# First pooling of a graph U-Net: turning the adjacency in 2-byte pairs of destinations, and picking the byte with two products per block

## The reference, cut to what matters

```python
def gcn_conv(x, W, b, src, dst, mask, n):
    h = x @ W
    ew = mask.astype(h.dtype)
    deg = 1.0 + jax.ops.segment_sum(ew, dst, num_segments=n)
    dinv = jax.lax.rsqrt(deg)
    norm = dinv[src] * dinv[dst] * ew
    agg = jax.ops.segment_sum(h[src] * norm[:, None], dst, num_segments=n)
    return agg + h * (1.0 / deg)[:, None] + b

def topk_pool(x, w, src, dst, mask, k):
    score = jnp.tanh((x * w).sum(-1) / jnp.sqrt((w * w).sum()))
    _, idx = jax.lax.top_k(score, k)
    n = x.shape[0]
    new_id = jnp.zeros((n,), jnp.int32).at[idx].set(jnp.arange(k, dtype=jnp.int32))
    kept = jnp.zeros((n,), bool).at[idx].set(True)
    mask2 = mask & kept[src] & kept[dst]
    return (x[idx], new_id[src], new_id[dst], mask2, idx)

# in the U-Net, i = 0, 1, 2:
    x = gcn_conv(x, dn_W[i], dn_b[i], src, dst, mask, n)
    x = jax.nn.relu(bn_train(x, dn_g[i], dn_beta[i]))
    k = int(RATIO * n)            # 3125 -> 1562 -> 781 -> 390
    x2, src2, dst2, mask2, idx = topk_pool(x, pool_w[i], src, dst, mask, k)
```

## Time and profile before

| | |
|---|---|
| median of 3 runs | 1019.72 us (1019.04 to 1021.31) |
| the profiled execution | 1018.97 us |
| its span, first to last instruction | 1017.0 us |
| granted TensorE clock, mean over the span | 0.978 |
| half turn, first product to last copy | 657.08 to 682.24 us |
| full turn, first product to last degree sum | 692.11 to 710.90 us |

### The profile page before, as it was taken

The page is one execution under the profiler, slowest core; times in us unless marked ns, Lnnn a source line. Parts: engine busy times, 40 slices in busy tenths (PEclk is TensorE's granted clock), DMA queues, the critical chain, the costliest instruction groups (busy, mean ns, idle before and its releaser), DMA issues.

```text
span 1017.0 us, 17626 instructions
## 1 busy us (share of the span) xinstructions
PE 907.3 (89%) x7247; PEld 601.0 (59%) x7247; DVE 590.3 (58%) x1557; ACT 401.2 (39%) x895; POOL 62.9 (6%) x84
## 2 busy tenths in 40 slices
PE   2347999999999999999999999998989687899997
PEld 1345666776765556775575576566545444456555
DVE  4789999995965972465212128384453464516311
ACT  0788999993554010165102013275214402122100
POOL 4000000000000000000000000404002200120000
PEclk9979999999899999999999999999999699999999
DMA  5010000003960002003000000784214300151002
GB/s 157 17 29 1 3 1 1 2 2 155 398 256 1 1 1 65 1 1 129 1 1 1 1 1 19 241 265 120 102 36 128 89 1 2 47 212 69 1 1 66
DMA packets 39505, 66.66 MB, mean 66 GB/s; under 512 B 3525, under 2 KB 27310, under 8 KB 38902
## 3 DMA queue, kind: packets, MB, share of 16 engines
q1 hardware_dynamic: 34464, 45.94, 13.1%
q0 software_dynamic: 4064, 17.86, 5.4%
q10 hardware_dynamic: 886, 1.61, 0.5%
HBM read 29.09 MB, written 36.32 MB: 64 GB/s over the span
## 4 chain that ended last, share of the span: by engine, by line
PE 61%; DVE 27%; ACT 4%; DMA 3%; issue 2%; POOL 1%; ACTq 0%; DVEq 0%; SPq 0%; POOLq 0%
PE psum L3121 26%; DVE region L1083 7%; PE psum L2616 7%; DVE region L1076 7%; PE psum L2504 7%; PE psum L2845 4%; DVE region L1681 2%; PE psum L2581 2%; PE psum L2409 2%; PE psum L2434 2%; PE psum L3069 1%; PE psum L2967 1%; DMA nodebuf<-in_x 1%; POOL region L839 1%; ACT nodebuf L2014 1%
## 5 line engine op out<-in xcount | busy, mean ns | idle before, releaser
L3121 PE MATMUL psum<-adj,region 128*128 128x448 fp8e4 (+1 forms) x1200 | 202.6, 329 | 1.1 <-DVE region L1920 1.0
L3121 PEld LDWEIGHTS psum<-adj,region 128*128 128x128 f16 x1200 | 116.5, 98 | 81.0 <-DVE region L1920 1.7
L2434 PE MATMUL psum<-region 128*128 128x200 bf16 (+2 forms) x1176 | 111.2, 229 | 27.3 <-DVE region L1083 19.0
L2434 PEld LDWEIGHTS psum<-region 128*128 128x128 bf16 x1176 | 93.4, 99 | 61.7 <-DVE region L1083 33.4
L1083 DVE TENSOR_TENSOR region<-iota_key,region 128x1200 bf16<-128x1200 bf16 x147 | 92.6, 702 | 0.0
L2071 ACT ACTIVATE adj<-psum 128x400 fp8e4<-128x400 f32 x196 | 86.5, 520 | 14.8 <-PE psum L2438 14.2
L2409 PE MATMUL psum<-adj,region 128*128 128x448 fp8e4 x350 | 92.1, 356 | 0.0
L1076 DVE TENSOR_TENSOR region<-iota_lo,region 128x3072 bf16<-128x3072 bf16 x49 | 86.9, 1774 | 5.2 <-PE psum L2438 5.0
L1948 DVE SCALAR_TENSOR_TENSOR region<-psum,unfit,region 128x448 f32<-128x448 f32 (+3 forms) x34 | 20.1, 622 | 107.7 <-PE psum L3121 98.4
L1681 DVE CAST region<-psum 128x512 fp8e4<-128x512 f32 (+2 forms) x87 | 46.6, 598 | 57.3 <-PE psum L2947 27.6
L3121 PE MATMUL psum<-region 128*128 128x448 fp8e4 (+3 forms) x452 | 76.8, 329 | 3.4 <-DVE region L1920 3.4
(11 more groups left out here) (376 smaller groups left out, 1268.6 us busy)
## 6 DMA issues: line engine op xcount, KB each, us to landing
both_table<-adj SPq DMA_DIRECT2D x1, 10000.0 KB, 28.7
adj_table<-adj SPq DMA_DIRECT2D x1, 10000.0 KB, 54.8
region<-dk_dram SPq DMA_DIRECT2D x2, 1568.0 KB, 7.3
both_table<-region SPq DMA_DIRECT2D x1, 2704.0 KB, 9.6
half_table<-region SPq DMA_DIRECT2D x2, 832.0 KB, 5.3
xs_dram<-nodebuf SPq DMA_DIRECT2D x1, 1600.0 KB, 5.2
nodebuf<-xs_dram SPq DMA_DIRECT2D x1, 1600.0 KB, 6.2
half_table<-region SPq DMA_DIRECT2D x2, 768.0 KB, 6.0
```

Source lines behind the costliest of these rows:

```text
L2434: pe.matmul(psum[:, q % BUILD_BANKS, i * KEYS + k0:i * KEYS + k1], hot_lo[:, r, c, j, :, i], hot_key[:, r, c, j, k0:k1, i], start=(n == 0) ...
L3121: last = pe.matmul(psum[:, b if b < BLOCKS else LAST_BANK, 0:width], here[:, t, k, :], rows, start=(t == 0 and k == 0), stop=(t == n_src - ...
```

## The change

- `adj` rows are read as 2-byte elements: destinations 2j and 2j+1 travel together. A row of 3200 bytes is 1600 elements, 12 tiles of 128 and one of 64 (`PAIR_TILES` 13, `PAIR_TAIL` 64).
- Half turn: 169 PE transposes of 2-byte elements (BF16 view, `ident16`) instead of 325 products. ACT and DVE copy them as 16-bit integers; a unit is 5 blocks (group 0) or 8 blocks (groups 1 and 2) of 128 elements; 27 units instead of 82. `half_table[0]` has 1664 lines of 3328 bytes, one for both destinations of a pair. It is still stored in six DMAs, now of 6 and 7 tiles.
- POOL gathers lines `node >> 1` (`node_of[:, 2]`), 3328 bytes each instead of 1664, 13 times 128 of them as before. They lie in other places of SBUF (`dst_block`).
- Full turn: of a gathered pair one byte is wanted. DVE makes two masks from the identity, `only_odd` (identity times the node's lowest bit) and `only_even` (the rest). For each block PE makes two products, the even bytes with one and the odd bytes with the other, in one PSUM sum: 338 products instead of 169.
- Both turns of this level use two banks per engine (3 and 4 for ACT, 5 and 7 for DVE), four in all.
- The skip sums move. Pass 0 (64 were left ahead of the half turn) goes 50 ahead of group 0 and 14 ahead of group 1; pass 1, now in bank 6, goes 14 ahead of group 2 and 36 between the turns. ACT's `take_skip(0)` moves behind the half turn, and the first degree sum waits for `take_skip(1)`, since it writes bank 6 too.

The second pooling keeps its form.

```diff
-TURN_BANKS = 3
+TURN_BANKS = (((3, 4), (5, 7)), ((0, 1, 2), (3, 4, 5)))
+PAIR_TILES = 13
+PAIR_TAIL = PAD // 2 - (PAIR_TILES - 1) * P
+def pair_ones():
+    return [(d, 1) for d in range(PAIR_TILES)]
+def pair_twos():
+    return [(d, min(2, PAIR_TILES - 1 - d)) for d in range(0, PAIR_TILES - 1, 2)] + [(PAIR_TILES - 1, 1)]
 def half_units(level):
+    if level == 0:
+        return [(g, d, count, 0, n) for g, (m0, n) in enumerate(store_groups(0)) for d, count in (pair_twos() if n <= 4 else pair_ones())]
...
 def half_parts(level):
+    if level == 0:
+        return ((0, 6), (6, PAIR_TILES))
...
+        half_table = [dram("half_table0", (PAIR_TILES * P, ROW[1] // 2), I32), dram("half_table1", (LEVEL_TILES[1] * P, ROW[2] // 4), I32)]
...
-        SKIP_PASSES = ((0, 0, 3, 0), (0, 3, 4, 7), (0, 4, BLOCKS, 0), (1, 0, 3, 0), (1, 3, 4, 3))
+        SKIP_PASSES = ((0, 0, 3, 0), (0, 3, 4, 6), (0, 4, BLOCKS, 0), (1, 0, 3, 0), (1, 3, 4, 3))
...
+                    if lv == 0:
+                        pool.wait_ge(pairs_known, 1)
                     for n in range(tiles_up):
-                        gather(dst_block(lv, n).bitcast(I32), half_table[lv], node_of[:, lv, n:n + 1], rows_gathered[n // 2])
+                        gather(dst_block(lv, n).bitcast(I32), half_table[lv], node_of[:, 2 - lv, n:n + 1], rows_gathered[n // 2])
...
+                    if level == 0:
+                        dve.wait_ge(nodes_known, 1)
+                        v.tensor_scalar(node_of[:, 2, :].bitcast(I32), node_of[:, 0, :].bitcast(I32), 1, None, ALU.arith_shift_right).then_inc(pairs_known, 1)
...
+                        dve.wait_ge(nodes_stored, DMA * len(NODE_STORES[0]))
...
+                        step(v.tensor_tensor(only_odd, every, odd.rearrange("p (t o) -> p t o", o=1).broadcast_to((P, packed_tiles, P)), ALU.mult))
+                        v.tensor_tensor(only_even, every, only_odd, ALU.subtract).then_inc(pairs_known, 1)
...
-                        take_skip((0, 2, 3)[below])
+                        if below > 0:
+                            take_skip((0, 2, 3)[below])
...
                                 if below == 0:
+                                    take_skip(0)
                                     take_skip(1)
...
+            SKIP_TURN, SKIP_LAST = ((86, 136), (136, 150)), 14
...
-                skip_sums(skips, SKIP_PICK[below][3], skip_sizes(skips))
+                if below > 0:
+                    skip_sums(skips, SKIP_PICK[below][3], skip_sizes(skips))
...
                 for u in range(turns(below)):
                     e, k, bank, _, _ = turn_unit(below, u)
+                    if below == 0 and (u == 0 or u < len(halves) and halves[u][0] != halves[u - 1][0]):
+                        pe.wait_ge(nodes_known, level)
+                        g = halves[u][0]
+                        if g < len(SKIP_TURN):
+                            skip_sums(0, *SKIP_TURN[g])
+                        if g == 2:
+                            skip_sums(1, 0, SKIP_LAST)
                     if u == len(halves):
                         pe.wait_ge(nodes_known, level)
                         if below == 0:
-                            skip_sums(1, 0, skip_sizes(1))
+                            skip_sums(1, SKIP_LAST, skip_sizes(1))
+                            pe.wait_ge(pairs_known, 2)
...
+                                if below == 0:
+                                    lanes = P if d < PAIR_TILES - 1 else PAIR_TAIL
+                                    at = ((d - d0) * n + m - m0) * P // 2
+                                    last = pe.transpose(psum[0:lanes, bank, at:at + P // 2].bitcast(BF16),
+                                                        src_block(0, m).bitcast(BF16)[:, d * P:d * P + lanes], ident16[:])
+                                    continue
...
+                            if below == 0:
+                                pairs = dst_block(0, n).bitcast(FP8).rearrange("p (s i) -> p s i", i=2)[:, m * P:(m + 1) * P, :]
+                                to = psum[:, bank, (m - m0) * P:(m - m0 + 1) * P]
+                                pe.matmul(to, pairs[:, :, 0], only_even[:, n, :], start=True, stop=False)
+                                last = pe.matmul(to, pairs[:, :, 1], only_odd[:, n, :], start=False, stop=True)
+                                continue
```

More of the change, by code:

```diff
@@ L30 @@
 U32 = mybir.dt.uint32
+U16 = mybir.dt.uint16
 P = 128
@@ L217, in gnn_kernel @@
         adj_table = dram("adj_table", (LEVEL_TILES[0] * P, ROW[0] // 4), I32)
-        half_table = [dram(f"half_table{lv}", (LEVEL_TILES[lv] * P, ROW[lv + 1] // 4), I32) for lv in range(PACKINGS)]
+        half_table = [dram("half_table0", (PAIR_TILES * P, ROW[1] // 2), I32), dram("half_table1", (LEVEL_TILES[1] * P, ROW[2] // 4), I32)]
         both_table = [dram(f"both_table{lv}", (LEVEL_TILES[lv] * P, BOTH_ROW[lv]), F32) for lv in range(PACKINGS)]
@@ L365, in gnn_kernel @@
         packed_adj.append(packed_adj[2])
-        half_at = ((3808, 7808), (6618, 8282), (6618, 7514))
+        half_at = ((3380, 7540), (6618, 8282), (6618, 7514))
+        only_even, only_odd = (r34(832 * k, 832).bitcast(F16).rearrange("p (t n) -> p t n", n=P) for k in range(2))
         node_rows = [r34(0, LEVEL_TILES[lv] * NODE_ROW[lv]).rearrange("p (t f) -> p t f", f=NODE_ROW[lv]) for lv in range(3)]
@@ L492, in gnn_kernel @@
         nodes_known = sem("nodes_known")
+        pairs_known = sem("pairs_known")
         rows_moved = relu_done = sem("rows_moved_or_relu_done")
@@ L609, in dst_block @@
         def dst_block(level, n):
-            at, words = gathered_dst[level]
-            return region12[:, at + n * words:at + (n + 1) * words]
+            if level == 1:
+                return region12[:, 3850 + n * 224:3850 + (n + 1) * 224]
+            return r34(3380 + 832 * n, 832) if n < 9 else region12[:, 832 * (n - 9):832 * (n - 8)]
         def up_block(level, t):
@@ L632, in turn_unit @@
             k = (before(ACT_TURNS, level) if e == 0 else before(DVE_TURNS, level)) + u // 2
-            bank = TURN_BANKS * e + k % TURN_BANKS
+            banks = TURN_BANKS[level][e]
+            bank = banks[u // 2 % len(banks)]
+            if level == 0 and u < len(halves):
+                g, d0, count, at, n = halves[u]
+                lanes = P if d0 + count < PAIR_TILES else PAIR_TAIL
+                to = half_rows(0, g).bitcast(U16)[0:lanes, d0:d0 + count, :]
+                return e, k, bank, to, psum[0:lanes, bank, 0:count * n * P // 2].bitcast(U16).rearrange("p (d n) -> p d n", d=count)
             if u < len(halves):
@@ L1858, in pick @@
                                     ).then_inc(nodes_known, 1)
+                    if level == 0:
+                        dve.wait_ge(nodes_known, 1)
+                        v.tensor_scalar(node_of[:, 2, :].bitcast(I32), node_of[:, 0, :].bitcast(I32), 1, None, ALU.arith_shift_right).then_inc(pairs_known, 1)
+                        parity = slot_parts[:, 0, 0:packed_tiles]
+                        step(v.tensor_scalar(parity, node_of[:, 0, :].bitcast(I32), 1, None, ALU.bitwise_and))
+                        odd = slots_of[:, 0, 0:packed_tiles]
+                        step(v.tensor_copy(odd, parity))
+                        dve.wait_ge(nodes_stored, DMA * len(NODE_STORES[0]))
+                        every = ident_h[:].rearrange("p (o n) -> p o n", o=1).broadcast_to((P, packed_tiles, P))
+                        step(v.tensor_tensor(only_odd, every, odd.rearrange("p (t o) -> p t o", o=1).broadcast_to((P, packed_tiles, P)), ALU.mult))
+                        v.tensor_tensor(only_even, every, only_odd, ALU.subtract).then_inc(pairs_known, 1)
                 def packed_degrees(level):
@@ L2908, in sum_degrees @@
                         pe.wait_ge(nodes_known, level)
-                        if below == 1:
+                        if below == 0:
+                            pe.wait_ge(skip_out, SKIP_OUT[1])
+                        else:
                             pe.wait_ge(skip_kept, SKIP_GROUPS[1])
@@ L2921, in pack @@
                         if below == 0:
-                            skip_sums(1, 0, skip_sizes(1))
+                            skip_sums(1, SKIP_LAST, skip_sizes(1))
+                            pe.wait_ge(pairs_known, 2)
                         else:
                             skip_rows()
-                    if k >= TURN_BANKS and e == 0:
-                        pe.wait_ge(act_turned, k - TURN_BANKS + 1)
-                    elif k >= TURN_BANKS:
-                        pe.wait_ge(dve_turned, k - TURN_BANKS + 1)
-                    if e == 0 and u // 2 < TURN_BANKS:
-                        pe.wait_ge(skip_out, (0 if below == 0 else SKIP_OUT[1]) + bank + 1)
+                    ring = len(TURN_BANKS[below][e])
+                    if u // 2 >= ring and e == 0:
+                        pe.wait_ge(act_turned, k - ring + 1)
+                    elif u // 2 >= ring:
+                        pe.wait_ge(dve_turned, k - ring + 1)
```

(2 more changed lines are left out.)

6 lines of the change are left out of this document (4 added, 2 removed).

## The result

The changed kernel took **1025.21 us** (median of 6 runs, 1022.80 to 1027.86), the kernel before 1019.38 us beside it (6 runs, 1017.77 to 1021.31): ratio **1.0053 [1.0039, 1.0066]**. It is slower, by 5.8 us in the medians. The forecast was 1020.3 us, with a range up to 1024.5. The profiled execution of the changed kernel took 1023.03 us, with a span of 1021.2 and a mean granted clock of 0.975; against the profiled execution of before it shows 4.1 us of the 5.8.

What follows compares the result with a forecast made beforehand. PE (89% busy) was taken to bound the kernel, the DMA the new half turn. Full turn starts 6.4 us earlier, 7.0 are lost in it: 1019.72 + 0.6 = 1020.3 us; own range 1018.5 to 1022, with rivals 1016 to 1024.5.

Steps and rivals of the forecast that it cites:

- The masks, priced at nothing: DVE ahead of the half turn's first copy: at most 2 x 1.9 us, covered by the wait for gathers, so 0.
- The half turn bound by the DMA, table at 679.6: From 658.7 on, 7.82 MB of gathers and stores at 383 GB/s take 20.4 us, plus half a microsecond for the receipt.
- Group 2: Last group of the half turn: waits for its gathers until 669.3, PE done at 672.3, last copy at 673.8.
- Transposes at 58 ns: Half turn on PE: each of the 169 2-byte transposes costs 58 ns, like products with 128 columns.
- rival C: Half turn: transposes cost 147 ns, PE bounds it, table near 690.8, total 1031.5 us; chance 0.09 together with Rival D.
- The copies of 640: Half turn, units of 640 columns: 0.70 us on ACT, 0.72 on DVE, with 0.36 as DVE's possible lower end.
- Second gather to first product 4.13 us: Between the turns: the old 3.43 us plus 0.7 for the second gather's doubled bytes, first product at 685.7.
- 683 to 688: Sign for the full turn's start: the forecast is wrong if it starts before 683 or after 688.
- Full turn 25.8 us: Tiles 1.80 us apart, bound by PE: 24.05 us plus 1.75 for the low clock, where the old turn took 18.8.
- Rival D: Full turn: products cost more than 58 ns; at 71 ns 4.4 us more, 1024.7 us; chance 0.09 together with rival C.
- The base: Old last degree sum at 710.90 in one profiled execution, with a full turn of 18.8 us; total 1019.72 us.
- Rival B: Half table's stores get only 305 GB/s: table at 683.4, full turn 689.5 to 715.3, 4.4 us lost, 1024.1 us; chance 0.20.

Runs made afterwards that it cites:

- masks_late: Changed kernel with its four mask instructions moved from ahead of the half turn to behind its last copy; 1024.27 us, ratio 1.0041 to the kernel before.
- extra_after: Changed kernel with one more store of 0.98 MB of unrelated data ahead of the half table's first store; 1029.07 us, ratio 1.0081 to the kernel before.
- late_spin: Changed kernel with masks behind the half turn's last copy and 34 idle products before the full turn; 1021.00 us, ratio 1.0017 to the kernel before.
- skip64: Changed kernel with all 64 skip sums of pass 0 ahead of group 0, as before the change; 1026.16 us, ratio 1.0054 to the kernel before.
- before_edge: Kernel before the change with six idle products ahead of PE's wait of 1.63 us near 840 us; 1018.66 us, ratio 1.0001 to the kernel before.

## Why the prediction was wrong

Three things failed: a term put at nothing (the masks), two terms of the DMA that were sized too small (the date of the table and the landing of the first gathers), and the base, one execution whose turn was 2 us longer than in the other profiles. Here are the steps, one by one, measured from t0 where executions are compared.

- **The masks, priced at nothing: wrong.** The prediction looked for who waits for DVE (nobody, until 655.5) and named the wait for the gathers as the cover. But the masks were what made that wait longer. They took POOL's first gather from 0.94 to 2.50 us. Group 0 started at 657.66, not 655.2, and PE waited 3.50 us, not 1.5; with the masks out of the way (masks_late) it waited 1.78. On the path this is 1.9 us (38.26 - 36.35).
- **The half turn bound by the DMA, table at 679.6: mechanism right** (extra_after), **size 1.2 us off.** That date is a first half gather at +35.1 (679.6 + 0.70 - 645.18). With the masks out of the way it comes at +36.35, +36.00 and +36.77. I took 383 GB/s from 658.7 on; from there to 681.0 the changed kernel moved 374, and masks_late and late_spin moved 367 and 372 from 658.2 until shortly before the end of their stores. So the stores with 1024 and 1280-byte pieces are much nearer to the gathers' pace than to 305, and the rate accounts for about half of the 1.2. The rest is the tail: the DMA share falls at 681.0 and the last store counts as landed at 682.6, 1.6 us later (0.8 to 0.9 in masks_late and late_spin), where I took 0.5.
- **Group 2: another wait than the one forecast.** I had it wait for its gathers until 669.3 (at an even split from 658.7 on, that sum should have given 670.6). It was turned from 671.61 on, without a wait for gathers, and what waited was its copies, 3.58 us on DVE for `half_rows` to come free of group 0's stores. They ended at 676.4, not 673.8. The DMA was full all the while, so this isn't on top of the item before.
- **Transposes at 58 ns: right.** 52 in 3.18 us, so rival C is out. The copies of 640 took 0.70 us on ACT, as forecast, and 0.49 on DVE, shorter than the 0.72 used. Off the path (skip64).
- **Second gather to first product 4.13 us: it was 5.19**, 689.95 - 684.76, in a DMA of 5.06 us. I had added 0.7 us for the doubled bytes; the measured addition is 1.8 (the other profiles in which PE waited for the gathers have 4.98 to 5.42 us for this step). It is a term mis-sized, 1.1 us. The first product stands at 689.95, outside the 683 to 688 that the prediction had named as the sign of being right.
- **Full turn 25.8 us: 25.2** (715.15 - 689.95), tiles 1.775 apart and no gap, clock at 0.50 up to 692.88. Right, the clock included. Rival D is out: the byte-wise weights and the shared sums cost nothing over 55.6 ns a product.
- **Sum of these:** +1.9 + 1.2 + 1.1 - 0.6 = 3.6 us, the whole difference between the forecast's end (711.5, or +66.3) and the measured one (+69.9).
- **The base.** 711.5 was set against 710.90 of one profiled execution, whose turn of 21.35 us held this wait for a gather, and then the clock at 0.50:
```profile
701.07 0.90 PE L2947 MATMUL psum<-ident_h,region 128*128 128x128 f16 x13 [1.97 <-DMA region<-half_table,node_of]
```
  The other three profiles of an unchanged turn have 19.2; their longest wait there is 0.67 to 1.01 us, and the clock stays at 1.00. The total of the first looked ordinary (1018.97) since it had luck elsewhere: no slow stretch near 843 us. I took a turn some 2 us too dear as that of before. So the forecast charged the new turn for the low clock and the old one as well, which cancelled; in the other profiles only the new one pays it. Both profiles compared in the result have no slow stretch near 843 us, and they differ by 4.2 us at the next level. Against the other three it would be some 6, which fits the 5.8 of the medians; how often either chance comes is not shown.

Against the three other profiles (next level at +66.3 to +67.0; here the +66.40 of before_edge) the account of the change is: 7.0 us for the second product, 1.4 for the cold clock, 1.8 for the longer way from POOL's gather to the first product (6.47 and 4.71), less 4.0 for the table that is there earlier (42.2 and 38.26): 6.2 later, and it is 6.1 (72.49 - 66.40).

Rival B had the place and nearly the price (first product 689.5, end 715.3), but by another cause: not stores at 305 GB/s, but gathers that start late, and 374 GB/s for gathers and stores together. That its date came true is luck.

Open: how often the executions of each kernel meet the slow stretch near 843 us and the gather wait of 2 us, since only profiled ones show it. The mean granted clocks hint at it (0.975 in the two fastest executions of the changed kernel, 0.970 to 0.974 in the four others), but they name no place. So the split of the 5.8 us is shown to about 1 us, not better. Whether 2-byte pairs can win at all was not tried beyond late_spin: its turn of 26.4 us is pure PE time, and 42.5 + 26.4 = 68.9 is above the 66.4 of before, so the table would have to come 2.5 us earlier still from a DMA that is full.

## What to carry to other kernels

Before a vector instruction is called free, ask not only who waits for it, but also whom it can hold up: one with two inputs in SBUF, running where POOL issues a gather, moved a whole DMA-bound stage by 1.9 us, and cost 0.5 to 0.8 in a stage bound by copies. Where a stage is traded from copies to DMA, what delays its first transfer comes onto the path. And before a sum goes against one profiled execution, look through the stretch at issue for waits that have nothing to do with its structure; a typical total doesn't make each of its parts typical.

## What the hardware showed that I had not expected

- An indirect gather of POOL ended 0.81 to 0.82 us behind the end of the DVE instruction with two SBUF inputs that ran as it was issued, in three kernels, with instructions of 1.89 and of 1.03 us.
- DVE copies 2-byte elements out of PSUM faster than 4-byte ones: 1024 columns of uint16 in 0.69 us, 512 of f32 in 0.69 as well. From 640 to 1024 columns of uint16 (0.49 to 0.69) that is 0.52 ns a column; from 128 to 512 of f32 (0.28 to 0.68) it is 1.05.
- The second gather of the half table took 5.06 us to land, with twice the bytes, where the first five of before took 3.1 to 3.3.
- A wait of PE of 1.63 us, then 49 tiny matmuls, then 0.48 us of waiting: around it the granted clock stayed at 1.00 in four executions and fell to 0.50 in six. In the five of these whose next 14 matmuls ran without a gap it cost them 1.3 to 2.6 us. A wait of 1.8 us ahead of group 0 did the same: the 65 transposes behind it took 4.22 us at 1.00 in late_spin and 5.68 at a mean of 0.70 in masks_late.
